# Attention, router and experts on one core: partitions that hold four consecutive tokens instead of one token of each tile

## The reference

```
xn   = layernorm(x)
q,k  = rope(xn @ Wq.T + bq), rope(xn @ Wk.T + bk)      # 16 heads of 16, angle = token number * theta
v    = xn @ Wv.T + bv
attn = softmax over 717 keys (the first 205 tokens and the last 512) of q k / 4, times v, then Wo, bo
ffn  = for each token the best of 8 experts (by router_w): silu(gate) * up, down (256 -> 176 -> 256),
       weighted with the softmax of its two best router logits
out  = x + attn + ffn
```

## Time and profile before

| | us |
|---|---|
| median of 3 runs | 376.69 (376.27 to 377.09) |
| the profiled execution, its own time | 375.99 |
| its span | 374.2 |
| PE busy | 365.2 |
| DVE busy | 327.7 |
| ACT busy | 269.1 |
| POOL busy | 72.3 |

### The profile page before, as it was taken

How to read it: one execution, slowest core, us unless ns; L and a number is a source line. 1 busy time by engine, 2 the same in 40 slices (tenths; PEclk the granted TensorE clock), 3 DMA queues, 4 the chain that set the end, 5 groups by cost and what they waited for, 6 DMA issues and landing times.

```text
span 374.2 us, 12333 instructions
## 1 busy us (share of the span) xinstructions
PE 365.2 (98%) x4702; PEld 204.3 (55%) x4702; DVE 327.7 (88%) x675; ACT 269.1 (72%) x546; POOL 72.3 (19%) x87
## 2 busy tenths in 40 slices
PE   8899899999999999999999999999999999999996
PEld 3655466766665564555545546455464554643365
DVE  5877889997768999999999999999999999998656
ACT  4736567564446888888888888888888888899920
POOL 3024824542000022020220202122122020210002
PEclk9999999999999999999999999999999999999999
DMA  7997856756310212222132221322313222111116
GB/s 231 297 372 290 261 164 215 218 163 168 110 54 30 59 33 61 63 75 74 35 84 70 58 68 39 91 77 58 88 32 93 62 56 76 32 39 39 25 35 228
DMA packets 32027, 40.46 MB, mean 108 GB/s; under 512 B 11108, under 2 KB 26468, under 8 KB 31520
## 3 DMA queue, kind: packets, MB, share of 16 engines
q1 hardware_dynamic: 29768, 34.42, 30.8%
q0 software_dynamic: 1872, 5.11, 5.0%
q10 hardware_dynamic: 336, 0.20, 0.3%
HBM read 25.65 MB, written 11.70 MB: 100 GB/s over the span
## 4 chain that ended last, share of the span: by engine, by line
PE 87%; DVE 4%; DMA 3%; ACT 2%; issue 2%; POOL 1%; SPq 0%; ACTq 0%; POOLq 0%; DVEq 0%
PE ps L822 22%; PE ps L852 21%; PE ps L747 14%; PE ps L698 6%; PE ps L760 6%; PE ps L711 5%; PE ps L830 3%; PE ps L736 2%; DMA o_st<-sorted_rows,token_of 2%; DMA x_sb<-x_in 2%; PE ps L612 1%; PE ps L723 1%; PE ps L601 1%; PE ps L684 1%; POOL o_st L513 1%
## 5 line engine op out<-in xcount | busy, mean ns | idle before, releaser
L1157 DVE TENSOR_REDUCE mx<-ps 128x1 f32<-128x512 f32 x232 | 150.7, 685 | 3.2 <-PE ps L747 0.7
L1487 ACT ACTIVATE probs<-ps 128x512 f32<-128x512 f32 x192 | 102.0, 598 | 19.0 <-PE ps L852 18.0
L852 PE MATMUL ps<-q_op,k_op 98*32 98x512 bf16 (+1 forms) x1104 | 112.1, 381 | 0.1
L747 PE MATMUL ps<-k_op,q_op 96*32 96x512 bf16 x672 | 76.1, 381 | 0.0
L1160 DVE TENSOR_REDUCE mx_tail<-ps 128x2 f32<-128x410 f32 x116 | 66.8, 576 | 3.4 <-PE ps L760 3.2
L852 PEld LDWEIGHTS ps<-q_op,k_op 98*32 98x32 bf16 (+1 forms) x1104 | 39.6, 96 | 33.0 <-issue 6.1
L822 PE MATMUL ps<-probs,v_op 128*32 128x512 f32 x384 | 52.4, 592 | 0.0
L519 POOL COPY v_op<-v_all 128x192 f32<-128x192 f32 x16 | 6.9, 437 | 188.3 <-PE ps L822 188.2
L1487 ACT ACTIVATE dn<-ps 77x512 f32<-77x512 f32 x64 | 34.3, 592 | 8.2 <-PE ps L852 8.2
L747 PEld LDWEIGHTS ps<-k_op,q_op 96*32 96x32 bf16 x672 | 25.0, 95 | 22.4 <-DVE mx L1157 8.0
L1487 ACT ACTIVATE gu<-ps 128x512 f32<-128x512 f32 x64 | 33.2, 604 | 4.9 <-PE ps L852 4.9
(11 more groups left out here) (148 smaller groups left out, 500.0 us busy)
## 6 DMA issues: line engine op xcount, KB each, us to landing
q_parts<-parts SPq DMA_DIRECT2D x12, 256.0 KB
sorted_results<-ys SPq DMA_DIRECT2D x23, 128.0 KB
gu<-gu_in SPq DMA_DIRECT2D x1, 2816.0 KB, 15.1
q_op<-q_parts SPq DMA_DIRECT2D x11, 192.0 KB, 3.2
sorted_rows<-xn SPq DMA_DIRECT2D x4, 512.0 KB, 11.7
xnT<-o_st SPq DMA_DIRECT2D x62, 32.0 KB, 2.0
tab<-softmax_recips SPq DMA_DIRECT2D x15, 128.0 KB
x_sb<-x_in SPq DMA_DIRECT2D x3, 512.0 KB, 6.8
```

The source lines that it names most:

```text
L747: ins = pe.matmul(bank(t % 2)[r:r + CW, :], q_op[slot][0:KR, P * t + r:P * t + r + CW], k_op[slot][0:KR, 0:NWIDE], start=True, stop=True)
L852: ins = pe.matmul(bank(4 + u % RING)[r:r + w, :], k_op[h % OPS][:, c0 + r:c0 + r + w], q_op[h % OPS][:, QB * b:QB * b + QB], start=True, s ...
L1157: dve.tensor_reduce(mx[:, slot, t:t + 1], bank(t % 2)[:, 0:NWIDE], AX.X, ALU.max).then_inc(wide_reduced, 1)
L1487: act.activation(prob[c][0:rows, QB * b:QB * b + QB], bank(4 + u % RING)[0:rows, :], ACT.Exp, scale=SCALE).then_inc(exp_done, 1)
```

## The change

In groups 1, 2 and 3 partition p now holds the tokens 512 g + 4 p to 512 g + 4 p + 3 in its four tiles. Group 0 stays as it was, since the first 205 keys end inside it. The function `tokens` gives the view of a DRAM array that belongs to a range of tiles, and the loads of x, the stores of `xn` and the stores of the result use it. A partition's part of a group of four tiles is then 4 KB in one piece in DRAM, instead of four pieces of 1 KB; for a pair of result tiles 2 KB.

The columns of `xnT`, and so of q and k, follow the new order, while the table `tab` stays in the order of the tokens. So for the units of groups 1 to 3 the two products with the table read it with a step of four floats: column 128 j + q of the unit takes table column 4 q + j. `token_id` is made by four iotas instead of one.

```diff
+        def tokens(ap, t0, t1):
+            g = t0 // 4
+            rows = ap[QB * g:QB * g + QB, :]
+            rows = rows.rearrange("(j p) d -> p j d", p=P) if g == 0 else rows.rearrange("(p j) d -> p j d", p=P)
+            return rows[:, t0 - 4 * g:t1 - 4 * g, :]
...
-            xv = x_d.rearrange("(t p) d -> p t d", p=P)
-            sp.dma_start(x_sb[:, 0:2, :], xv[:, 0:2, :]).then_inc(x_first, 16)
+            sp.dma_start(x_sb[:, 0:2, :], tokens(x_d, 0, 2)).then_inc(x_first, 16)
             for g in range(4):
                 t0 = 4 * g if g else 2
-                sp.dma_start(x_sb[:, t0:4 * g + 4, :], xv[:, t0:4 * g + 4, :]).then_inc(x_in[g], 16)
+                sp.dma_start(x_sb[:, t0:4 * g + 4, :], tokens(x_d, t0, 4 * g + 4)).then_inc(x_in[g], 16)
...
-                sp.dma_start(nv[:, 4 * g:4 * g + 4, :], xn[:, 4 * g:4 * g + 4, :]).then_inc(xn_stored, 16)
+                sp.dma_start(tokens(xn_dram, 4 * g, 4 * g + 4), xn[:, 4 * g:4 * g + 4, :]).then_inc(xn_stored, 16)
...
-                sp.dma_start(ov[:, t0:t1, :], x_sb[:, t0:t1, :]).then_inc(out_stored, 16)
+                sp.dma_start(tokens(out_d, t0, t1), x_sb[:, t0:t1, :]).then_inc(out_stored, 16)
...
-            pool.iota(token_id[:], [[P, NT]], base=0, channel_multiplier=1).then_inc(iota_ready, 1)
+            pool.iota(token_id[:, 0:4], [[P, 4]], base=0, channel_multiplier=1).then_inc(iota_ready, 1)
             pool.wait_ge(iota_ready, 2)
+            for g in range(1, 4):
+                pool.iota(token_id[:, 4 * g:4 * g + 4], [[1, 4]], base=QB * g, channel_multiplier=4
+                          ).then_inc(iota_ready, 1)
+                pool.wait_ge(iota_ready, g + 2)
...
             def over_odds(u, fn):
                 t0, n = PROJ[u][1:3]
-                return tab[:, fn:fn + 1, t0:t0 + n].broadcast_to([P, 2, n])
+                if t0 < QB:
+                    return tab[:, fn:fn + 1, t0:t0 + n].broadcast_to([P, 2, n])
+                return tab[:, fn:fn + 1, t0:t0 + n].rearrange("p a (q j) -> p a j q", j=4
+                                                              ).broadcast_to([P, 2, 4, P])
+
+            def blocks(u, ap):
+                return ap if PROJ[u][1] < QB else ap.rearrange("p a (j q) -> p a j q", j=4)
...
-                dve.tensor_tensor(rot_of(u, 0), rot_of(u, 1), over_odds(u, 0), ALU.mult).then_inc(cos_ready, 1)
+                dve.tensor_tensor(blocks(u, rot_of(u, 0)), blocks(u, rot_of(u, 1)), over_odds(u, 0), ALU.mult).then_inc(cos_ready, 1)
...
-                dve.tensor_tensor(rot_of(u, 1), rot_of(u, 1), over_odds(u, 1), ALU.mult).then_inc(sin_ready, 1)
+                dve.tensor_tensor(blocks(u, rot_of(u, 1)), blocks(u, rot_of(u, 1)), over_odds(u, 1), ALU.mult).then_inc(sin_ready, 1)
```

More of the change, by code:

```diff
@@ L351, in store_part @@
                 sp.dma_start(dst, parts[:, u % 2, part, :, 0:n]).then_inc(parts_stored[u % 2], 16)
-            nv = xn_dram.rearrange("(t p) d -> p t d", p=P)
             for g in range(4):
@@ L485, in _ @@
                     load_last_recip(sp, half, b)
-            ov = out_d.rearrange("(t p) d -> p t d", p=P)
             for n, (t0, t1) in enumerate(OUT_TILES):
                 sp.wait_ge(out_ready, n + 1)
-                sp.dma_start(ov[:, t0:t1, :], x_sb[:, t0:t1, :]).then_inc(out_stored, 16)
+                sp.dma_start(tokens(out_d, t0, t1), x_sb[:, t0:t1, :]).then_inc(out_stored, 16)
             sp.wait_ge(out_stored, 16 * len(OUT_TILES))
@@ L499, in _ @@
             pool.wait_ge(iota_ready, 1)
-            pool.iota(token_id[:], [[P, NT]], base=0, channel_multiplier=1).then_inc(iota_ready, 1)
+            pool.iota(token_id[:, 0:4], [[P, 4]], base=0, channel_multiplier=1).then_inc(iota_ready, 1)
             pool.wait_ge(iota_ready, 2)
+            for g in range(1, 4):
+                pool.iota(token_id[:, 4 * g:4 * g + 4], [[1, 4]], base=QB * g, channel_multiplier=4
+                          ).then_inc(iota_ready, 1)
+                pool.wait_ge(iota_ready, g + 2)
             pool.tensor_copy(lane16, lane).then_inc(iota_ready, 1)
-            pool.wait_ge(iota_ready, 3)
+            pool.wait_ge(iota_ready, 6)
             pool.wait_ge(logits_T_ready, 1)
@@ L1084, in slot_of_tokens @@
                     over_slots(row_slot[:]), ALU.is_equal))
-                dve.wait_ge(iota_ready, 3)
+                dve.wait_ge(iota_ready, 6)
                 settle()
```

## The result

The changed kernel takes 383.77 us (median of 6 runs, 381.50 to 384.97) against 376.71 us (6 runs) for the kernel before: 7.06 us more, a ratio of 1.0173 with a 95% interval of 1.0147 to 1.0198. The forecast was 379.9, with 377.0 to 382.2 as range: the direction was right, the size forecast (3.2 us) less than half, and the median lies above the range.

What follows compares the result with a forecast made beforehand. PE, busy 98% of the span, was taken as the bound. 0.64 (unit 1) + 2.84 (units 3 to 5) - 0.20 (x) - 0.10 (stores) = +3.18 us, carried to the median 379.9 us, range 377.0 to 382.2.

Steps and rivals of the forecast that it cites:

- the price of a product: DVE's cos and sin products of units 1, 3, 4, 5: each 0.70 us more for the strided table read.
- the credit: At 82.35 us DVE waits 0.66 us for ACT; this was taken to absorb that much of units 3 to 5's lag.
- -0.4, -0.2 and -0.1 us: Larger packets: table part 1 lands 0.4 us earlier, x's group 1 load gains 0.2, the last stores 0.1.
- L1066 over L1041: Rows for pricing the stride: the reduction's 0.70 ns a column was taken, not the scalar operation's 0.28.
- The rival that the step of four floats is free: DVE's strided products cost nothing extra, leaving only the x and store gains: 376.4 us; chance 0.14.
- Net 1.40 - 0.40 - 0.36 = 0.64 us: PE's wait at 40.99: two longer products, less the earlier table and an absorbed gather wait, delay PE 0.64 us.
- The credit of 0.40 us for an earlier table: Unit 1's chain: larger packets bring table part 1 0.4 us earlier, offsetting part of the longer products.
- 3.50 less the 0.66: DVE's full stretch: five products lag 3.50 us, less its 0.66 us idle time; PE leaves 2.84 us late.
- The sixth, `times_cos(3)`: Unit 3's cos product, before 52.82 us: its lag is free up to DVE's 0.85 us wait for ACT.
- from 66 us on: PE's weight loads at L736 would already wait for DVE's late maxima from 66 us, not only at 84.44.
- 0.64 + 2.84 - 0.30 = 3.2: Whole kernel: unit 1's delay plus that of units 3 to 5, less x and store gains, +3.18 us.

Runs made afterwards that it cites:

- e1: The changed kernel with the table's columns laid out in the order of the partitions, so products read adjacent floats: 377.12 us, ratio 0.9994.
- e14: The changed kernel with the table in partition order and ACT's row copy for slot 1 ahead of the cast, table issued as before: 376.22 us, ratio 0.9993.
- e9: The kernel before plus unused DVE products and copies at its end, at steps of 1 to 16 floats: 1.22 us at step 2, 0.75 more at 4.
- e5: The kernel before with only unit 1's two products reading the table at a step of four floats: 379.62 us, ratio 1.0071.
- e6: The kernel before with only the six products of units 3, 4 and 5 reading at a step of four floats: 381.40 us, ratio 1.0109.
- e12: The changed kernel, table part 2 issued after slot 3's gather and ACT's row copy for slot 1 ahead of the cast: 381.82 us, ratio 1.0131.
- e3: The changed kernel with table part 2 issued only when the gather for slot 3, not slot 1, has landed: 383.25 us, ratio 1.0152.
- e2: The kernel before, own layout and 1 KB packets, with the table laid out so the same eight products read it strided: 384.62 us, ratio 1.0202.

## Why the prediction was right and wrong

**The bound, and where to look.** Right: from 96 us on PE is as full as before, and all of the loss lies in two places of the first 93 us, the wait near 41 us and the full stretch of DVE. Of the miss of 3.9 us (3.2 forecast, 7.06 measured) unit 1 has 2.1, units 3 to 5 have 1.3 (0.6 by the price of a product, 0.7 by the credit), and the packets 0.3; the small rest is within the noise.

**Packets.** The sum had -0.4, -0.2 and -0.1 us. The wait for x fell from 0.48 to 0.26 us and the table came 0.38 us earlier in the profiled execution. But both vary by more than that from run to run: with the same loads of x the wait was 0.16 us in e1 and 0.84 in e14, and the table's landing is spread over 2.1 us. e1 gives 0.9994 (0.9975 to 1.0014) for all packets together: worth nothing measurable, which agrees with the rows that gave 1 KB packets and those of 2 to 8 KB about the same rate.

**The price of a strided product.** 0.70 us taken, 0.81 measured in the kernel and 0.75 alone in e9: mis-sized by a seventh. The choice of row was right, L1066 over L1041. The reason given for it fits e9, which does not prove it: the step of four adds 0.38 us to the copy with one source (1.07 for 0.69) and 0.75 to the product. The rival that the step of four floats is free (chance 0.14) was wrong.

**Unit 1: the step that failed.** "Net 1.40 - 0.40 - 0.36 = 0.64 us" followed one chain, through ACT's row copy, and took PE's wait there as the sum of what was late. Alone, unit 1 costs 2.7 us (e5), and 4.3 in the profiled execution. Two costs were missing. The gather for slot 2 runs on POOL beside the product and waits for its end (shown); it then landed late, it seems behind 1.25 MB of table and `wo` (suggested by the trace, not tested). The prediction priced POOL's iotas but not its gathers. And behind the long wait TensorE was granted its lower level, 1.8 us in the profile, which was in no term of the sum. The credit of 0.40 us for an earlier table has nothing to show for it either, by e1. The row copy came 1.2 us late, near the 1.0 us worked out. How the 2.7 us divide between the two links, the clock and DVE's lag stays open.

**Units 3 to 5: the second step that failed.** "3.50 less the 0.66" gave 2.84 us; measured are 4.0 in the profile and 4.1 in e6. Five products at 0.81 are 4.05: of these nothing was absorbed. The sixth, `times_cos(3)`, was free, as forecast: the sine after it begins at 57.67 us for 53.45 before, 4.2 later, no more than the first place had cost by then. DVE's idle 0.66 us is there again at 90.60, because ACT's cast, for which DVE waits, stands in ACT's order right behind the copy of turned rows (81.00 and 81.27 us before, 89.26 and 89.53 after, each 8.3 later), and those rows come from DVE's own gated products by way of PE. So the cast was as late as DVE. An idle time of DVE behind a wait that shifts with the same lag is no slack. The path to PE was in part another one than forecast, too. Weight loads of the tiles do wait for maxima, but first at 78.74 (0.50 us) and at 84.67 (0.56), not from 66 us on, and they cost PE 0.16 us; the experts' chain cost it 2.48 us. The prediction had left out that the gated products stand in the same full queue of DVE.

**The sum.** Predicted 0.64 + 2.84 - 0.30 = 3.2, measured 2.7 + 4.1 in the two separate kernels, 7.06 together. That the two add was right, though e12 points at a limit: without the early stop part of unit 1's lag reaches PE later.

## What to carry to other kernels

A layout that makes transfers prettier is paid where its order is undone: here eight vector products with a step of 16 bytes, each two thirds longer, for packets whose worth could not be measured. If the order of a table has to change, change it where the table is laid out. Before a lag is credited against an idle time, ask whether that idle time would move with the lag; and when a vector operation gets longer, look at what POOL does beside it, not only at who waits for its result.

## What the runs showed of the hardware

- A float32 product on DVE with one operand at a step of 2 floats takes 1.22 us for 1024 columns, as at a step of 1; at a step of 4 it takes 1.97, and steps of 8 and 16 cost about the same per column. The Trainium skill ("Vector Engine (DVE) Microarchitecture Reference", Measured stream behaviour on trn2) has 1.73 ns a column for one source that hops 4 KiB every element, which is within about 5% of the 1.72 to 1.82 here; its condition, pairs of adjacent words, is stricter than what e9 shows, where a step of 2 has none and is at full rate. The Trainium skill ("SBUF — State Buffer", the note on cachelines) has a step of 4 floats as free; the runs contradict it for DVE. What the same note says before that, that two hits in a 16-byte line are needed for the full rate, agrees with the steps tried.
- POOL's indirect gather waits for the end of DVE's product that runs beside it, and then ends 0.81 to 0.84 us later. Alone it took 0.95 us, beside short pieces 1.24 to 1.30, beside one long product 2.43, and in one execution 4.60 behind a row of operations without a gap.
- After PE had waited 4.20 us near 40 us in the changed kernel's profile, the granted clock was 0.57 from 44 to 48 us; after 3.01 us in e3's it was 0.50 there. In e2's profile it stayed at 1.0 after 2.99 us, so the wait's length alone does not tell. The mean clock of four of six executions of the changed kernel was 0.994 to 0.995, that of the other two 0.999.
